# The order of VectorE's steps in a supertile of a two-layer graph network: weighting and part sums first, addition of finished sums behind them

## The chip, the cores and the metric

The kernel runs on one core of one Trainium2 chip. The metric is the device time of one execution in microseconds (us). The engines are TensorE (PE, its weight loads PEld), VectorE (DVE), ScalarE (ACT), GpSimd (POOL) and SyncE (SP). They run their own instruction queues and wait for each other by semaphores.

## The reference, cut to what matters

Two message-passing layers run over the same graph of 6250 nodes and 206250 edges, sorted by their destination `dst`. For each edge a row of its source node is taken, combined with four edge attributes (`sh`), scaled by a function of 16 edge scalars, and summed into the destination node:

```python
# layer 0, per edge
out_s = (einsum(xs[src] * es, W_ss) / sqrt(64) + einsum(xv[src], ev, W_vv) * ISQ3 / sqrt(32)) * ISQ2
out_v = (einsum(xs[src], ev, W_sv) * ISQ3 / sqrt(64) + einsum(xv[src], es, W_vs) * ISQ3 / sqrt(32)) * ISQ2
messages = concatenate([out_s, out_v]) * sigmoid(edge_scalars @ W_rad.T + b_rad)
agg = segment_sum(messages, dst)
# layer 1, per edge: h = silu(edge_scalars @ Wfc1), w = h @ Wfc2; e0, e1 = rows of the source
mid0 = w0 * e0 * sh0
mid1 = w3 * einsum(e1, sh1) / sqrt(3)
mid2 = w1 * e0 * sh1
mid3 = w2 * e1 * sh0
# segment means of them, then node products; each layer ends in a layer norm over 160 columns
```

All of it is float32.

## The kernel before, in words

The edges are cut into 404 supertiles of 512 (four tiles of 128, one edge to a partition). The weight products are made once for each node, ahead of the edges, in a table in DRAM: rows of 448 floats for layer 0, of 224 for layer 1. So an edge needs its source's row, weighted by its own attributes. The two edge layers are the same loop (`edge_layer`, L670 on VectorE, L929 on TensorE) with other bodies. A round is four supertiles; the loop runs over 101 rounds. What each engine does with supertile s:

- GpSimd (`gathers_of_round`, L370) gathers the rows: four indirect DMAs (L361), one for each tile, into one of four buffers (`rows0`, in the trace `arena`; `rows1`, in the trace `work`). It refills the buffer of supertile s with the rows of s + 4 when both ScalarE (`s_wtd`, L373) and VectorE (`s_wone`, L375) have weighted supertile s.
- ScalarE weights most of the row by the edge's attributes (L433, 12 instructions, `s_wtd`), when the messages of s - 2 are made (L441, L450), since they share a buffer; in layer 0 it then applies the sigmoid to TensorE's radial product (L459, `s_act`), in layer 1 the silu for s + 1 (L517). In layer 0 a part (`s_whead`) is done first, to which VectorE adds.
- TensorE waits for the messages of s (L947, L919), makes the radial product of s + 2 in layer 0 (L883, `s_lin`), and then sums the messages of s by destination (L907, `s_agg`): a matmul with a one-hot matrix of each tile over one window of 128 nodes, into one of two PSUM banks. In layer 1 the products for s + 1 and s + 2 (L900, L892) come ahead of the sums. Some supertiles have edges in further windows (about one in eight): `further` on both sides.
- VectorE turns the destinations into floats (L704), adds the sums that TensorE made of supertile s - 2 into `acc` (`add_sums`, L668; it waits for `s_agg`, L705), weights what ScalarE left (`weight_by_one`, L600: L609 in layer 0, L612 in layer 1, four instructions, `s_wone`), makes the one-hots (`select`, L657, L660, `s_oh`), and the messages (`messages0`, L616: two part sums at L625, then the product with the sigmoid's result at L632; `messages1`, L634: a part sum at L645, then L647, L648, L651, L652, L655). The last one signals `s_msg`.
- SyncE (`loads_behind`, L297) loads the small arrays: `escal` behind `s_lin`, `dst_sh` (destinations and attributes of two supertiles) behind the additions (L305), `srcs` once a round behind the gathers.

The order on each engine is written out by hand as the order of its queue; a wait holds up everything behind it on that engine. The sums of two supertiles have a bank each, the one-hots and the messages two buffers each, so a bank is added two supertiles behind its sums, ahead of the one-hots that reuse that buffer.

Of the kernel before, what the change touches and what calls it, by code (L numbers as in the profile page):

```python
# [6 lines left out]
MS, MV = 64, 32  # L7
# [33 lines left out]
DEEP0 = 2  # L41
# [6 lines left out]
def mk_gnn_resnorm_d2_gnn_r8_694f30_kernel(nc, a):  # L48
    f32, bf16, i32, i16 = mybir.dt.float32, mybir.dt.bfloat16, mybir.dt.int32, mybir.dt.int16
    ALU = mybir.AluOpType  # L50
# [3 lines left out]
    with ctx:  # L54
# [13 lines left out]
        msg0 = arena[:, at:at + 2 * TPS * MSG0].rearrange("p (s t c) -> p s t c", s=2, t=TPS)  # L68
# [6 lines left out]
        weighted1 = work[:, at1:at2].rearrange("p (s t c) -> p s t c", s=2, t=TPS)  # L75
        weighted0 = work[:, 0:DEEP0 * TPS * PARTS0].rearrange("p (s t c) -> p s t c", s=DEEP0, t=TPS)
# [37 lines left out]
        half = sb("half", [P, TPS, 2, MS])  # L114
# [29 lines left out]
        rad = [two_to_a_bank(2 * b, DIM) for b in range(2)]  # L144
# [37 lines left out]
        s_wtd = [sem(f"rows_weighted{l}") for l in range(2)]  # L182
# [373 lines left out]
        def _(dve):  # L556
# [43 lines left out]
            def weight_by_one(l, s, i, j):  # L600

                dve.wait_ge(s_rows[l][j], (i + 1) * 16 * TPS)
                if l == 0:
                    dve.wait_ge(s_whead, s + 1)
                for t in range(TPS):
                    scale = dst_sh[:, j, TPS + 4 * t + 2:TPS + 4 * t + 3]
                    if l == 0:
                        to = weighted0[:, j % DEEP0, t, 128:224]
                        last = nc.vector.scalar_tensor_tensor(to, rows0[:, j, t, 0:96], scale.bitcast(f32), to,  # L609
                                                              ALU.mult, ALU.add)  # L610
                    else:
                        last = nc.vector.tensor_scalar(weighted1[:, j % 2, t, 448:544], rows1[:, j, t, 128:224],  # L612
                                                       scale.bitcast(f32), None, ALU.mult)
                last.then_inc(s_wone[l], 1)

            def messages0(s, j):  # L616

                u, m, c = weighted0[:, j % DEEP0, :, :], msg0[:, j % 2, :, :], rad[j % 2]
                dve.wait_ge(s_wone[0], s + 1)
                dve.wait_ge(s_wtd[0], s + 1)  # L620

                def summed(to, at, k):

                    parts = u[:, :, at:at + k * P].rearrange("p t (k c) -> p t k c", k=k)
                    nc.vector.tensor_reduce(to, parts[:, :, :, 0:MS].rearrange("p t k c -> p t c k"),  # L625
                                            AX.X, ALU.add).then_inc(s_part[0], 1)

                summed(u[:, :, 0:MS], 160, 3)
                summed(u[:, :, MS:2 * MS], 224, 2)
                dve.wait_ge(s_part[0], s * 2 + 2)  # L630
                dve.wait_ge(s_act[0], s + 1)
                nc.vector.tensor_tensor(m[:, :, 0:DIM], u[:, :, 0:DIM], c, ALU.mult).then_inc(s_msg[0], 1)  # L632

            def messages1(s, j):  # L634


                u, m, w, h = weighted1[:, j % 2, :, :], msg1[:, j % 2, :, :], wps[j % 2], half

                def blocks(x, n):
                    return x.rearrange("p t (k c) -> p t k c", k=n)  # L640

                dve.wait_ge(s_wone[1], s + 1)
                dve.wait_ge(s_wtd[1], s + 1)

                nc.vector.tensor_tensor(h[:, :, 0, 0:MV], u[:, :, 224:256], u[:, :, 416:448], ALU.add).then_inc(s_part[1], 1)  # L645
                dve.wait_ge(s_w2, s + 1)
                nc.vector.tensor_tensor(m[:, :, 0:MS], u[:, :, 32:96], w[:, :, 0:64], ALU.mult)  # L647
                nc.vector.tensor_tensor(blocks(m[:, :, 96:192], 3), blocks(u[:, :, 0:288], 3)[:, :, :, 0:MV],  # L648
                                        bc(w[:, :, 128:160], 2, [P, TPS, 3, MV]), ALU.mult)
                dve.wait_ge(s_part[1], s * 2 + 1)  # L650
                nc.vector.tensor_tensor(h[:, :, 1, 0:MV], h[:, :, 0, 0:MV], u[:, :, 512:544], ALU.add).then_inc(s_part[1], 1)  # L651
                nc.vector.tensor_tensor(blocks(m[:, :, 192:384], 3), blocks(u[:, :, 256:544], 3)[:, :, :, 0:MS],  # L652
                                        bc(w[:, :, 64:128], 2, [P, TPS, 3, MS]), ALU.mult)
                dve.wait_ge(s_part[1], s * 2 + 2)
                nc.vector.tensor_tensor(m[:, :, 64:96], h[:, :, 1, 0:MV], w[:, :, 160:192], ALU.mult).then_inc(s_msg[1], 1)  # L655
# [14 lines left out]
            def edge_layer(l):  # L670
                LAST = NODE_TILES - 1
                waiting, newer = dve.alloc_register(f"window_to_add{l}"), dve.alloc_register(f"window_after{l}")
                waiting_more, visit = dve.alloc_register(f"more_to_add{l}"), dve.alloc_register(f"further_visit{l}")

                def held(register):
                    return dve.snap(register, min_val=0, max_val=LAST)  # L676

                dve.reg_mov(waiting, 0)  # L680
                dve.reg_mov(newer, 0)
                dve.reg_mov(waiting_more, 0)
                dve.reg_mov(visit, 1)
                dve.sem_inc(s_add[l], 1)
                dve.sem_inc(s_addx[l], 1)

                def next_visit():
                    return dve.snap(visit, min_val=1, max_val=SUPS * NODE_TILES)

                def further(s, j, window, k):  # L690
                    e = next_visit()
                    dve.wait_ge(s_aggx[l], e)
                    dve.wait_ge(s_addx[l], e)
                    dve.wait_ge(s_add[l], s + 2)
                    add_sums(l, MORE, held(waiting_more)).then_inc(s_addx[l], 1)
                    at = dve.snap(window + k + 1).with_bounds(min_val=1, max_val=LAST)
                    dve.reg_mov(visit, e + 1)
                    dve.wait_ge(s_addx[l], next_visit())
                    select(j, 2, at).then_inc(s_ohx[l], 1)
                    dve.reg_mov(waiting_more, at)  # L700

                def supertile(s, i, j, window, more):
                    dve.wait_ge(s_dsh[l][j // PAIR], (i + 1) * 16)
                    nc.vector.tensor_copy(dstf[:, j % 2, :], dst_sh[:, j, 0:TPS]).then_inc(s_dstf[l], 1)  # L704
                    dve.wait_ge(s_agg[l], s + 1)  # L705
                    dve.wait_ge(s_add[l], s + 1)
                    add_sums(l, FIRST + j % 2, held(waiting)).then_inc(s_add[l], 1)
                    weight_by_one(l, s, i, j)
                    dve.wait_ge(s_dstf[l], s + 1)
                    select(j, j % 2, window).then_inc(s_oh[l], 1)  # L710
                    (messages0, messages1)[l](s, j)
                    with dve.If(more > 0):
                        further(s, j, window, 0)
                        with dve.If(more > 1):
                            with dve.Fori(1, more) as k:
                                further(s, j, window, k)
                    dve.reg_mov(waiting, held(newer))
                    dve.reg_mov(newer, window)

                with dve.Fori(0, ROUNDS) as i:  # L720
                    _, values = nc.values_load_multi_w_load_instructions(  # L721
                        wtab[0:1, bass.ds(i, 1), 0:2, :], engines=[dve.engine], min_val=0, max_val=LAST,
                        skip_runtime_bounds_check_because="a dst is a node's number, so its window is one of the tiles")
                    for j in range(SLOTS):
                        supertile(i * SLOTS + j, i, j, values[j], values[SLOTS + j])

                for k, window in enumerate((waiting, newer)):
                    dve.wait_ge(s_agg[l], SUPS + k + 1)
                    dve.wait_ge(s_add[l], SUPS + k + 1)
                    add_sums(l, FIRST + k, held(window)).then_inc(s_add[l], 1)  # L730
                e = next_visit()
                dve.wait_ge(s_aggx[l], e)
                dve.wait_ge(s_addx[l], e)
                dve.wait_ge(s_add[l], SUPS + 3)
                add_sums(l, MORE, held(waiting_more)).then_inc(s_addx[l], 1)
                dve.reg_mov(visit, e + 1)
                dve.wait_ge(s_addx[l], next_visit())
                dve.sem_inc(s_done[l], 1)
# [426 lines left out]
```

## Time and profile before

| | |
|---|---|
| time, median of 3 runs | 5723.65 us (5711.29 to 5736.86) |
| the profiled execution's own time | 5735.73 us |
| its span, first to last instruction | 5733.9 us |
| mean granted TensorE clock | 0.699 of full speed |
| PE busy | 3993.3 us (70%) |
| DVE busy | 3889.5 us (68%) |
| ACT busy | 3382.4 us (59%) |
| POOL busy | 3141.9 us (55%) |

The span has a short opening, layer 0's edges up to about 2725 us, some 110 us of node work, layer 1's edges from about 2840 to 5650 us, and an end. The views below take 500 to 2600 us as a stretch of layer 0 and 3000 to 5500 us as a stretch of layer 1. Of a PE matmul the trace has the time at which it is taken up; its end is modelled. A row of a timeline gives the start, the time taken, engine and line, output and inputs, the count, and in brackets how long the engine was idle before it and who released it. "remote" is a release by an engine or a queue that the profile can't name.

### The profile page before, as it was taken

The numbers are of one execution on the slowest core, as the hardware profiler recorded it, in microseconds if no ns is written. First come the engines' busy times: TensorE is split into PE (matmuls) and PEld (weight loads), VectorE is DVE, ScalarE is ACT, GpSimd is POOL, SyncE is SP. The second block draws the span as 40 slices with busy tenths as digits, with TensorE's granted clock in tenths as the row PEclk, the third lists the DMA queues.
The fourth block names the chain that finished last, engine by engine and source line by source line (L and its number), as shares of the span: only waits on it lengthen the run. The fifth ranks groups of instructions, "written<-read, shape, count | busy, mean of one in ns | idle before, by whom it ended". The sixth has DMA issues, their size and how long they took to land.

```text
span 5733.9 us, 82997 instructions
## 1 busy us (share of the span) xinstructions
PE 3993.3 (70%) x16478; PEld 2635.1 (46%) x16479; DVE 3889.5 (68%) x12732; ACT 3382.4 (59%) x10841; POOL 3141.9 (55%) x3275
## 2 busy tenths in 40 slices
PE   5656565656566566666777777777777777777877
PEld 4445454545455455545544443444444344444435
DVE  4676777777777767777566666666666666666667
ACT  4666666666666666666555555555555555555555
POOL 4555555555555555555355555555555555555551
PEclk7555555555555555555888888888888888888888
DMA  7555555555555555555222222222222222222221
GB/s 239 150 147 154 148 152 148 152 148 154 146 150 152 148 151 148 151 149 133 79 76 76 75 74 74 73 75 74 75 73 74 76 76 78 75 74 76 77 76 51
DMA packets 325631, 641.98 MB, mean 112 GB/s; under 512 B 143598, under 2 KB 175131, under 8 KB 325499
## 3 DMA queue, kind: packets, MB, share of 16 engines
q0 software_dynamic: 181584, 557.89, 35.6%
q1 hardware_dynamic: 144016, 83.72, 5.6%
q8 instruction: 14, 0.23, 0.0%
q14 instruction: 17, 0.14, 0.0%
HBM read 620.47 MB, written 20.88 MB: 112 GB/s over the span
## 4 chain that ended last, share of the span: by engine, by line
PE 34%; DVE 28%; another core or an unknown queue 16%; issue 12%; ACT 6%; DVEq 3%; DMA 1%; ACTq 0%; POOL 0%; SPq 0%
PE ps L907 22%; DVE work L625 9%; DVE onehot L660 5%; ACT work L433 5%; DVE work L609 5%; PE ps L900 4%; PE ps L883 3%; PE ps L892 3%; DVE arena L632 1%; DVE work L612 1%; DVEq L676 1%; DVE work L648 1%; DVEq L721 1%; PE ps L870 1%
## 5 line engine op out<-in xcount | busy, mean ns | idle before, releaser
L361 POOL DMA_INDIRECT work<-table,srcs x1616 | 1559.9, 965 | 1237.8 <-issue 511.1
L361 POOL DMA_INDIRECT arena<-table,srcs x1616 | 1537.2, 951 | 1137.8 <-DVE work L609 619.3
L433 ACT ACTIVATE work<-arena,dst_sh 128x96 f32<-128x96 f32 (+1 forms) x4848 | 1415.7, 379 | 430.8 <-DVE arena L632 379.2
L907 PE MATMUL ps<-work,onehot 128*128 128x384 f32 x3616 | 1535.0, 578 | 180.6 <-DVE work L655 129.8
L433 ACT ACTIVATE work<-work,dst_sh 128x96 f32<-128x96 f32 (+1 forms) x4848 | 1499.6, 398 | 23.6 <-issue 10.8
L883 PE MATMUL ps<-wrad,escal 17*128 17x160 f32 x3232 | 561.2, 494 | 1033.9 <-DVE arena L632 857.5
L907 PEld LDWEIGHTS ps<-work,onehot 128*128 128x128 f32 x3616 | 771.3, 223 | 854.7 <-issue 524.7
L907 PE MATMUL ps<-arena,onehot 128*128 128x161 f32 x3616 | 1082.8, 479 | 12.3 <-issue 9.2
L907 PEld LDWEIGHTS ps<-arena,onehot 128*128 128x128 f32 x3616 | 925.0, 320 | 140.6 <-issue 131.2
L883 PEld LDWEIGHTS ps<-wrad,escal 17*128 17x128 f32 x3232 | 405.7, 309 | 1189.8 <-issue 840.6
L517 ACT ACTIVATE hid<-ps 128x256 f32<-128x256 f32 x404 | 152.0, 376 | 1180.6 <-remote 924.6
L660 DVE TENSOR_SCALAR onehot<-iota,dstf 128x128 f32 x3616 | 790.6, 287 | 16.4 <-issue 9.2
L900 PE MATMUL ps<-fc,hid 64*128 64x192 f32 x3232 | 422.9, 385 | 453.7 <-ACT hid L517 346.1
L668 DVE TENSOR_TENSOR arena<-arena,ps 128x384 f32 x455 | 251.1, 552 | 663.0 <-remote 320.2
L625 DVE TENSOR_REDUCE work<-work 128x256 f32<-128x768 f32 (+1 forms) x808 | 656.6, 854 | 0.0
L900 PEld LDWEIGHTS ps<-fc,hid 64*128 64x128 f32 x3232 | 290.4, 210 | 712.3 <-ACT hid L517 410.2
L459 ACT ACTIVATE ps<-ps 128x640 f32<-128x640 f32 x404 | 276.5, 684 | 563.0 <-remote 483.9
L668 DVE TENSOR_TENSOR acc<-acc,ps 128x161 f32 x455 | 145.7, 320 | 673.9 <-remote 340.0
L609 DVE SCALAR_TENSOR_TENSOR work<-arena,dst_sh,work 128x96 f32<-128x96 f32 x1616 | 406.3, 312 | 0.0
L652 DVE TENSOR_TENSOR work<-work,ps 128x768 f32<-128x768 f32 x404 | 382.2, 946 | 0.0
L612 DVE TENSOR_SCALAR work<-work,dst_sh 128x96 f32<-128x96 f32 x1616 | 337.4, 284 | 5.7 <-DMA work<-table,srcs 5.7
L632 DVE TENSOR_TENSOR arena<-work,ps 128x640 f32<-128x640 f32 x404 | 331.7, 821 | 14.0
(122 smaller groups left out, 2057.7 us busy)
## 6 DMA issues: line engine op xcount, KB each, us to landing
escal<-in_escal SPq DMA_DIRECT2D x404, 98.0 KB
arena<-table,srcs POOLq DMA_INDIRECT x1616
work<-table,srcs POOLq DMA_INDIRECT x1616
table<-work SPq DMA_DIRECT2D x49, 224.0 KB, 2.6
dst_sh<-in_dst_sh SPq DMA_DIRECT2D x404, 20.0 KB
table<-work SPq DMA_DIRECT2D x7, 784.0 KB, 4.0
acc<-in_xd SPq DMA_DIRECT2D x1, 3920.0 KB
arena<-in_xd SPq DMA_DIRECT2D x7, 560.0 KB, 4.1
```

Of the source, the lines that this page charges most:

```text
L361: pool.indirect_dma_start(out=rows[:, j, t, :], out_offset=None, in_=table, in_offset=bass.IndirectOffsetOnAxis(ap=srcs[:, b, j, t:t + 1], ...
L433: last = nc.scalar.activation(u[:, t, to:to + c1 - c0], r[:, t, c0:c1], ACT.Copy, scale=dst_sh[:, j, at:at + 1].bitcast(f32))
L609: last = nc.vector.scalar_tensor_tensor(to, rows0[:, j, t, 0:96], scale.bitcast(f32), to, ALU.mult, ALU.add)
L612: last = nc.vector.tensor_scalar(weighted1[:, j % 2, t, 448:544], rows1[:, j, t, 128:224], scale.bitcast(f32), None, ALU.mult)
L625: nc.vector.tensor_reduce(to, parts[:, :, :, 0:MS].rearrange("p t k c -> p t c k"), AX.X, ALU.add).then_inc(s_part[0], 1)
L632: nc.vector.tensor_tensor(m[:, :, 0:DIM], u[:, :, 0:DIM], c, ALU.mult).then_inc(s_msg[0], 1)
L652: nc.vector.tensor_tensor(blocks(m[:, :, 192:384], 3), blocks(u[:, :, 256:544], 3)[:, :, :, 0:MS], bc(w[:, :, 64:128], 2, [P, TPS, 3, MS]) ...
L660: last = nc.vector.tensor_scalar(onehot[:, b, t, :], iota[:, bass.ds(window * P, P)], dstf[:, j % 2, t:t + 1], None, ALU.is_equal)
L668: return nc.vector.tensor_tensor(to, to, bank(b)[:, 0:n], ALU.add)
L883: last = mm(rad[j % 2][:, t, :], escal[r, j, t % 2 * P:(t % 2 + 1) * P], wrad[r, :], start=True, stop=True)
L900: last = mm(wps[j % 2][:, t, :], hid[h, j % 2, t % 2 * P:(t % 2 + 1) * P], fc2[h, :], start=True, stop=True)
L907: last = mm(bank(to)[:, 0:(MSG0, MSG1)[l]], onehot[:, b, t, :], m[:, j % 2, t, :], start=t == 0, stop=t == TPS - 1)
```

## The change

Only VectorE's queue changes. `weight_by_one` and the first part of the messages, which is cut off as `parts0` (L618 to L629) and `parts1` (L642 to L645), go ahead of the wait for TensorE's sums. The new order in a supertile is: destinations as floats, weighting, part sums, addition of the sums of s - 2, one-hots, rest of the messages. The instructions, their operands, the semaphores and all other engines' queues are the same.

```diff
--- before.py
+++ after.py
@@ -613,9 +613,9 @@
                                                        scale.bitcast(f32), None, ALU.mult)
                 last.then_inc(s_wone[l], 1)
 
-            def messages0(s, j):
-
-                u, m, c = weighted0[:, j % DEEP0, :, :], msg0[:, j % 2, :, :], rad[j % 2]
+            def parts0(s, j):
+
+                u = weighted0[:, j % DEEP0, :, :]
                 dve.wait_ge(s_wone[0], s + 1)
                 dve.wait_ge(s_wtd[0], s + 1)
 
@@ -627,22 +627,28 @@
 
                 summed(u[:, :, 0:MS], 160, 3)
                 summed(u[:, :, MS:2 * MS], 224, 2)
+
+            def messages0(s, j):
+
+                u, m, c = weighted0[:, j % DEEP0, :, :], msg0[:, j % 2, :, :], rad[j % 2]
                 dve.wait_ge(s_part[0], s * 2 + 2)
                 dve.wait_ge(s_act[0], s + 1)
                 nc.vector.tensor_tensor(m[:, :, 0:DIM], u[:, :, 0:DIM], c, ALU.mult).then_inc(s_msg[0], 1)
 
+            def parts1(s, j):
+
+                u = weighted1[:, j % 2, :, :]
+                dve.wait_ge(s_wone[1], s + 1)
+                dve.wait_ge(s_wtd[1], s + 1)
+                nc.vector.tensor_tensor(half[:, :, 0, 0:MV], u[:, :, 224:256], u[:, :, 416:448], ALU.add).then_inc(s_part[1], 1)
+
             def messages1(s, j):
-
 
                 u, m, w, h = weighted1[:, j % 2, :, :], msg1[:, j % 2, :, :], wps[j % 2], half
 
                 def blocks(x, n):
                     return x.rearrange("p t (k c) -> p t k c", k=n)
 
-                dve.wait_ge(s_wone[1], s + 1)
-                dve.wait_ge(s_wtd[1], s + 1)
-
-                nc.vector.tensor_tensor(h[:, :, 0, 0:MV], u[:, :, 224:256], u[:, :, 416:448], ALU.add).then_inc(s_part[1], 1)
                 dve.wait_ge(s_w2, s + 1)
                 nc.vector.tensor_tensor(m[:, :, 0:MS], u[:, :, 32:96], w[:, :, 0:64], ALU.mult)
                 nc.vector.tensor_tensor(blocks(m[:, :, 96:192], 3), blocks(u[:, :, 0:288], 3)[:, :, :, 0:MV],
@@ -702,10 +708,11 @@
                 def supertile(s, i, j, window, more):
                     dve.wait_ge(s_dsh[l][j // PAIR], (i + 1) * 16)
                     nc.vector.tensor_copy(dstf[:, j % 2, :], dst_sh[:, j, 0:TPS]).then_inc(s_dstf[l], 1)
+                    weight_by_one(l, s, i, j)
+                    (parts0, parts1)[l](s, j)
                     dve.wait_ge(s_agg[l], s + 1)
                     dve.wait_ge(s_add[l], s + 1)
                     add_sums(l, FIRST + j % 2, held(waiting)).then_inc(s_add[l], 1)
-                    weight_by_one(l, s, i, j)
                     dve.wait_ge(s_dstf[l], s + 1)
                     select(j, j % 2, window).then_inc(s_oh[l], 1)
                     (messages0, messages1)[l](s, j)
```

## Rows read from the trace of the kernel before

**Rows 1.** Windows of both edge layers: us, busy us (instructions) of PE, PEld, DVE, ACT, POOL, clock, DMA.

```profile
500.00:2600.00 2100.00, 1286.30 (x5447) 1060.30 (x5447) 1486.20 (x4373) 1322.12 (x4181) 1220.94 (x1284) 0.53 0.55 150
3000.00:5500.00 2500.00, 1943.20 (x7528) 1019.77 (x7527) 1658.69 (x5967) 1430.40 (x4674) 1386.57 (x1436) 0.83 0.28 75
```

**Rows 2.** Waits of DVE, layer 0: waiter <- releaser: us in total, times, longest us.

```profile
DVE acc L668 <- remote: 272.7, 94, 7.7
DVE acc L668 <- PE ps L907: 244.1, 62, 5.5
```

**Rows 3.** Waits of DVE, layer 1.

```profile
DVE arena L668 <- remote: 283.6, 80, 7.7
DVE arena L668 <- PE ps L907: 240.9, 91, 5.1
...
DVE half L645 <- ACT work L433: 61.1, 44, 2.1
```

**Rows 4.** Timeline of layer 0, 1529 to 1543 us.

```profile
1529.40 1.44 PE L883 MATMUL ps<-wrad,escal 17*128 17x160 f32 x8 [1.63 <-DVE arena L632]
...
1530.76 2.52 PE L907 MATMUL ps<-arena,onehot 128*128 128x161 f32 x8
...
1535.85 0.95 POOL L361 DMA_INDIRECT arena<-table,srcs  x1 [0.30 <-issue]
1538.45 0.69 ACT L459 ACTIVATE ps<-ps 128x640 f32<-128x640 f32 x1 [5.64 <-remote]
1538.67 0.32 DVE L668 TENSOR_TENSOR acc<-acc,ps 128x161 f32 x1 [4.83 <-PE ps L907]
1538.91 1.00 DVE L609 SCALAR_TENSOR_TENSOR work<-arena,dst_sh,work 128x96 f32<-128x96 f32 x4
1539.05 3.49 ACT L433 ACTIVATE work<-arena,dst_sh 128x160 f32<-128x160 f32 x12
...
1539.82 0.87 DVE L660 TENSOR_SCALAR onehot<-iota,dstf 128x128 f32 x4
...
1540.61 1.63 DVE L625 TENSOR_REDUCE work<-work 128x256 f32<-128x768 f32 x2
1540.69 0.94 POOL L361 DMA_INDIRECT arena<-table,srcs  x1 [3.89 <-DVE work L609]
...
1542.27 0.82 DVE L632 TENSOR_TENSOR arena<-work,ps 128x640 f32<-128x640 f32 x1
```

**Rows 5.** Timeline of layer 0, 1614 to 1626 us.

```profile
1614.53 2.52 PE L907 MATMUL ps<-arena,onehot 128*128 128x161 f32 x8
...
1622.08 0.94 POOL L361 DMA_INDIRECT arena<-table,srcs  x1 [0.30 <-issue]
...
1625.15 0.32 DVE L668 TENSOR_TENSOR acc<-acc,ps 128x161 f32 x1 [7.56 <-remote]
```

**Rows 6.** Timeline of layer 1, 4215 to 4223 us.

```profile
4215.75 0.95 POOL L361 DMA_INDIRECT work<-table,srcs  x1 [0.30 <-issue]
...
4218.16 0.56 DVE L668 TENSOR_TENSOR arena<-arena,ps 128x384 f32 x1 [3.93 <-PE ps L907]
...
4220.23 1.02 POOL L361 DMA_INDIRECT work<-table,srcs  x1 [3.53 <-DVE work L612]
...
4222.20 0.28 DVE L655 TENSOR_TENSOR work<-half,ps 128x128 f32<-128x128 f32 x1
```

**Rows 7.** Waits of POOL, layer 0.

```profile
POOL arena L361 <- DVE work L609: 500.5, 217, 4.6
```

**Rows 8.** Waits of POOL, layer 1.

```profile
POOL work L361 <- DVE work L612: 341.0, 184, 4.3
POOL work L361 <- ACT work L433: 310.2, 99, 7.0
```

**Rows 9.** Waits of ACT, layer 0.

```profile
ACT ps L459 <- remote: 401.8, 102, 7.2
```

**Rows 10.** DMA issues of the page: count, KB each, us from issue to landing.

```profile
table<-work SPq DMA_DIRECT2D x49, 224.0 KB, 2.6
```

## The prediction, made before the change was run

> **What bounds the kernel now.** I read the view of windows first. Nothing is full in either edge layer: in layer 0 VectorE is busy 1486.2 of 2100 us and GpSimd's issuing 1220.9 us, in layer 1 TensorE 1943.2 of 2500 us [rows 1]. Four gathers go out for a supertile, so the issues count supertiles: 1284/4 = 321 in 2100 us (6.54 us each) and 1436/4 = 359 in 2500 us (6.96 us each). So a loop of waits bounds both layers.
>
> The waits of VectorE name its link. In layer 0 VectorE stands 272.7 + 244.1 = 516.8 us in 156 waits before L668, the addition of sums that TensorE made two supertiles before [rows 2]; in layer 1 it is 524.5 us in 171 waits, and the weighting by ScalarE makes it wait only 61.1 us at L645 [rows 3].
>
> The timeline says what kind of wait this is. The sums wanted at 1538.67 were in TensorE's queue at 1530.76 and by their record over at 1533.28, so the signal comes 5.4 us after the work. ScalarE's sigmoid wakes at 1538.45, for a product that began at 1529.40 and took 1.44. Two signals of different age arrive together. What comes before both is GpSimd's last gather issue at 1535.85: 2.8 us earlier [rows 4]. A second place: VectorE stands from 1617.59, GpSimd still has gathers to issue up to 1622.08, and the wait lasts 7.56 us, again until 3.1 us after the last issue, although the sums were over at 1617.05 [rows 5]. In layer 1 the last issue is at 4215.75 and the wait ends at 4218.16, 2.4 us later [rows 6]. I take it that TensorE's signals are **held back while a run of gathers goes on**, and come some 2.4 to 3.1 us after its last issue.
>
> GpSimd in turn stops because it has no permission: it wants the weighting of a supertile before it refills that buffer. It waits 500.5 us in 217 pauses on VectorE's L609 in layer 0 [rows 7]; in layer 1 it is 341.0 us in 184 pauses on L612 and 310.2 us in 99 on ScalarE [rows 8]. So the loop is: signal late, VectorE stands, no weighting, GpSimd stops, signal comes, VectorE weights, GpSimd goes on. The bookkeeping closes: 321 x 4 x 1.25 us (an issue of 0.95 and 0.30 between, [rows 4]) + 500.5 = 2106 of 2100 us, and 359 x 5.0 + 651.2 = 2446 of 2500 us.
>
> **The change, part by part.** No instruction is added or removed: 808 supertiles do the same work. Moved ahead of the wait on the sums are VectorE's weighting (1.00 us in layer 0, 0.80 in layer 1) and the part sums (L625, 1.63 us; L645, 0.28 us) with their waits on rows and on ScalarE.
>
> 1. Behind a late signal less is left. In layer 0 the addition starts at 1538.67 and the messages end at 1543.09: 4.42 us. Taken out: from 1538.91 to 1539.82 the weighting (0.91), from 1540.61 to 1542.27 the part sums (1.66). Left 1.85 us [rows 4]. In layer 1 it is 4.32 us (4218.16 to 4222.20 + 0.28) [rows 6], less 0.71 and 0.20, left 3.41. Upper bound of the gain: 2.57 and 0.91 us for each wait, 156 x 2.57 = 401 and 171 x 0.91 = 156 us in the two stretches. Lower bound: nothing, if the signal comes later by as much.
>
> 2. GpSimd's permission now comes before VectorE stands, so a run of gathers can be longer by one supertile (5.0 us), and by the reading above the signal is later by up to 5.0 us. The second place is the nearest row: with some 4.5 us of issues left the wait was 7.56 us instead of 4.83 or 3.93 [rows 4 to 6]. I take this in full.
>
> 3. The next permission comes later behind the signal. Now GpSimd resumes 1540.69 - 1538.67 = 2.0 us behind the addition [rows 4]. After: 1.85 us to the messages, 0.2 to the next supertile, 1.00 of weighting, 0.8 from its end to the issue (1539.91 to 1540.69): 3.85 us. Where ScalarE stood too, its sigmoid (0.69) and its 3.49 us of weights [rows 4] come first: about 4.4. ScalarE stands at the sigmoid in 102 of the waits [rows 9], so I take the mean, 4.1: a pause is 2.1 us longer. In layer 1: 3.41 + 0.2 + 0.80 + 0.8 = 5.2 instead of 2.1 (4218.16 to 4220.23), 3.1 us longer, but only at the 184 pauses that VectorE ends.
>
> 4. Fewer, longer pauses. Layer 0 has 321/217 = 1.48 supertiles to a pause of 500.5/217 = 2.31 us. One more for part 2, and 0.25 more because in a longer pause some sums get through that are held now (bounds: none, and every second one): 2.73. Then 321/2.73 = 118 pauses x 4.4 = 519 us against 500.5: +18, and for all 404 supertiles +23 us. Layer 1 has 359/283 = 1.27. Only the 184 of 283 pauses (0.65) get the further supertile: 1.27 + 0.65 + 0.25 = 2.17, 165 pauses x 4.31 us (0.65 x (341.0/184 + 3.1) + 0.35 x 310.2/99) = 711 against 651.2: +60, for 404 supertiles +68 us.
>
> 5. The rest lies beside other work. SyncE's loads of dst_sh wait for the addition, which now leaves 1.85 us instead of 4.4 to the messages that let ScalarE start on that buffer; the landing isn't shown, and the nearest row, 2.6 us for a store of 224 KB [rows 10], would cost ScalarE 0.8 us in every second supertile, hidden unless ScalarE is the last. Take 0; the upper end is 404 x 0.8 = 323 us, unlikely since ScalarE has over a third of its time idle [rows 1]. Its loads of escal and srcs behind it are rounds ahead. One-hots are later, but TensorE waits for the messages first and these still end the supertile. L645 now waits for ScalarE before the addition instead of behind it: 61.1 us of waiting [rows 3] lose their cover of 1.3 us each in 44 cases, 57 us at most, which I count in rival C. All GpSimd and VectorE durations are taken as they are.
>
> Sum: 23 + 68 = +91 us on the profiled execution's 5735.73 us: 5827. That execution is 12 us above the median of the runs, 5723.65, so against the median 5815; I say **5815 us**.
>
> The Trainium skill ("SBUF — State Buffer", section Who interferes with whom) speaks against part 2: it says that a DMA never contends with a compute engine and that only VectorE and GpSimd share a port. By that rule gathers can't delay TensorE's signals and rival A is the outcome. Rows 4 to 6 show signals that come together and behind the last issue, which that rule doesn't explain.
>
> **Rivals.** A, the plain gain: the signals are late by themselves and GpSimd's issues have no part in it. Then the whole of part 1 comes off: 401 x 404/321 = 505 us and 156 x 404/359 = 176 us, at most 681; the shortest waits are shorter than 2.57 us, so about 600: 5125 us. For it: the wait in rows 4 is longer than the work moved. Against it: the wait of 7.56 us, and three waits that end so alike behind GpSimd's last issue.
>
> B, faster through fewer pauses. Same mechanism, but in the longer pause after a signal (GpSimd starts 3.85 to 5.2 us behind it) the next sums get through nearly always: the messages are there at 1.85 us, product and sums take 1.44 + 2.52 us [rows 4], so 5.8 us in layer 0. It decides for this when more than about one in two gets through. With each one: layer 0 1.48 + 2 = 3.48, 92 pauses x 4.4 = 405, -95 us, for the layer -120; layer 1 1.27 + 0.65 + 1 = 2.92, 123 x 4.31 = 530, -121, for the layer -136. 5724 - 256 = 5470 us. Against it: GpSimd has begun again before 5.8 us.
>
> C, slower by more: none gets through (2.48 and 1.92 supertiles to a pause). 129 x 4.4 = 568, +67, +85 for the layer; 187 x 4.31 = 806, +155, +174 for the layer. With 57 us for L645: 5724 + 85 + 174 + 57 = 6040 us.
>
> **Chances.** Own forecast 0.45 (range 5690 to 5930), A 0.13, B 0.22, C 0.20. Faster or slower means beyond 0.5%, or 29 us, which is about what a measurement of this kernel can tell. Faster: A, B and a hair of the own range (0.02): 0.37. Same: 0.11, all of it in the own range. Slower: 0.32 of the own, and C: 0.52. The range leaves out A and a few of C's worst: 5400 to 6030 us.
>
> **What the profile after would show.** Part 1: from the addition to the messages' end 1.85 us in layer 0 and 3.4 in layer 1. Part 2: VectorE's waits before L668 still end 2.4 to 3.1 us behind GpSimd's last issue, and in layer 0 are as long as now or longer, but fewer. Parts 3 and 4: GpSimd's pauses number some 120 instead of 217 in 2100 us and last over 4 us. Wrong if the waits before L668 shrink to under half with GpSimd's runs grown together (A), or if the pauses are fewer than 100 (B). Waiting at L645 or L609 on ScalarE of over 150 us would speak for C.

## The result, and the profile after

The changed kernel takes **5915.8 us** (median of 4 runs, 5898.4 to 5952.0), beside 5717.5 us for the kernel before (5707.6 to 5736.9): ratio 1.034 [1.032, 1.037], +198 us. The direction is as forecast and the time lies in the range of 5400 to 6030 us, but the forecast +91 us are less than half of the +198 measured. The profiled executions differ by less: 5898.35 - 5735.73 = +162.6 us, as that of after is the lowest of its runs (17 us under their median) and that of before 18 us above its own.

Where the time went, from the start of the first messages to the end of the last in each layer (worked out from the two traces; in layer 1 up to the last messages' first product, L647 before and L653 after): layer 0 2628.5 us before and 2721.0 after, **+93**; layer 1 2799.7 and 2871.0, **+71**. The sum, +164, is the whole difference of the profiled executions. Forecast were +23 and +68.

The windows of both layers, as in [rows 1]:

```profile
500.00:2600.00 2100.00, 1228.04 (x5282) 1011.90 (x5284) 1428.69 (x4240) 1267.02 (x4044) 1190.62 (x1244) 0.54 0.53 145
3000.00:5500.00 2500.00, 1914.16 (x7364) 1004.48 (x7364) 1654.82 (x5840) 1392.09 (x4569) 1348.59 (x1406) 0.83 0.28 73
```

1244 issues are 311 supertiles (6.75 us each, 6.54 before), 1406 are 351.5 (7.11 us, 6.96 before). Every engine is less busy: more waiting, not more work. The granted clock is what it was. VectorE's waits in layer 0 answer to [rows 2], to which a third group of the kernel before belongs: waits for which the profile shows no releaser ("issue"). It comes first here:

```profile
DVE acc L668 <- issue: 21.8, 9, 3.1
```

```profile
DVE acc L674 <- remote: 478.8, 82, 10.6
DVE acc L674 <- issue: 72.8, 18, 7.4
DVE work L625 <- remote: 36.9, 18, 4.7
DVE acc L674 <- PE ps L914: 28.4, 13, 2.8
```

The waits before the addition (now L674) are fewer and longer: 580.0 us in 113 instead of 516.8 + 21.8 = 538.6 in 165, up to 10.6 us instead of 7.7. GpSimd's waits in layer 0, to be held against [rows 7]:

```profile
POOL arena L361 <- issue: 506.3, 1082, 7.9
POOL arena L361 <- DVE work L609: 345.2, 104, 9.1
POOL arena L361 <- ACT work L433: 35.1, 43, 8.0
```

Part of the pauses is now in the first group (its longest is 7.9 us, though the common gap is 0.30). Counted in the trace from 500 to 2700 us as the time above the usual 1.25 us from issue to issue, where it is over 0.35 us, 220 pauses of 2.31 us became **130 of 4.25 us** (124 to 140 with a limit of 0.5 or 0.3 us; before the limit makes no difference). ScalarE, against [rows 9]:

```profile
ACT ps L459 <- remote: 673.7, 90, 14.2
```

One place in the timeline of layer 0 shows the new order at work, with a signal on time and one held:

```profile
1519.31 0.32 DVE L674 TENSOR_TENSOR acc<-acc,ps 128x161 f32 x1
1519.54 0.88 DVE L666 TENSOR_SCALAR onehot<-iota,dstf 128x128 f32 x4
...
1520.32 0.82 DVE L636 TENSOR_TENSOR arena<-work,ps 128x640 f32<-128x640 f32 x1
...
1528.27 0.94 POOL L361 DMA_INDIRECT arena<-table,srcs  x1 [0.30 <-issue]
1528.38 0.32 DVE L674 TENSOR_TENSOR acc<-acc,ps 128x161 f32 x1 [4.57 <-remote]
...
1531.29 0.69 ACT L459 ACTIVATE ps<-ps 128x640 f32<-128x640 f32 x1 [4.81 <-remote]
1531.51 1.00 DVE L609 SCALAR_TENSOR_TENSOR work<-arena,dst_sh,work 128x96 f32<-128x96 f32 x4
...
1533.30 0.95 POOL L361 DMA_INDIRECT arena<-table,srcs  x1 [4.09 <-DVE work L609]
```

From the addition to the messages' end are 1520.32 + 0.82 - 1519.31 = 1.83 us, 4.42 before. The sigmoid at 1531.29 comes 3.0 us behind the last issue, as in [rows 4 to 6]; the addition at 1528.38 got its signal sooner, within 0.1 us of that issue. So the hold isn't strict: some signals slip through. GpSimd stands 4.09 us until it is given the weighting of 1531.51.

The end of a matmul is modelled, so these rows alone can't tell a late signal from late work. ScalarE's end is measured, and its signal is held too. Here its weighting is over at 1503.92 + 3.49 = 1507.41, and VectorE, which waits for it before the part sums, starts at 1513.33, together with ScalarE's sigmoid and 3.0 us behind the last gather issue:

```profile
1503.92 3.49 ACT L433 ACTIVATE work<-arena,dst_sh 128x160 f32<-128x160 f32 x12
...
1510.32 0.95 POOL L361 DMA_INDIRECT arena<-table,srcs  x1 [0.30 <-issue]
...
1513.33 1.03 DVE L625 TENSOR_REDUCE work<-work 128x256 f32<-128x768 f32 x1 [4.70 <-remote]
1513.42 0.69 ACT L459 ACTIVATE ps<-ps 128x640 f32<-128x640 f32 x1 [6.01 <-remote]
```

The update of ScalarE's semaphore is recorded 0.09 us before VectorE starts, 5.8 us behind the end of the work. So what is late is the signal, and not TensorE's alone. From 500 to 2600 us, 61 recorded updates of this semaphore are over 0.3 us late, 22 in the kernel before.

VectorE's and GpSimd's waits in layer 1, against [rows 3] (again with the third group of before, which comes first) and [rows 8]:

```profile
DVE arena L668 <- issue: 59.9, 36, 5.1
```

```profile
DVE arena L674 <- remote: 254.7, 54, 8.0
DVE half L643 <- ACT work L433: 224.5, 109, 6.8
DVE work L653 <- remote: 178.5, 49, 7.5
...
DVE half L643 <- issue: 43.8, 28, 4.4
DVE arena L674 <- PE ps L914: 28.5, 18, 3.1
DVE arena L674 <- issue: 18.2, 10, 4.7
```

```profile
POOL work L361 <- ACT work L433: 419.4, 93, 7.2
POOL work L361 <- DVE work L612: 156.9, 77, 8.6
```

Here the wait moved. Before the addition it fell from 524.5 + 59.9 = 584.4 to 254.7 + 28.5 + 18.2 = 301.4 us, but L643 (L645 before) now waits 224.5 us for ScalarE instead of 61.1. ScalarE waits for another product of TensorE's, held in the same way. In the timeline the last issue is at 4212.72, and ScalarE (L517) and VectorE's L653 wake together 2.8 to 2.9 us behind it:

```profile
4212.72 0.96 POOL L361 DMA_INDIRECT work<-table,srcs  x1 [0.30 <-issue]
...
4215.56 0.42 DVE L653 TENSOR_TENSOR work<-work,ps 128x256 f32<-128x256 f32 x1 [1.40 <-remote]
4215.62 0.38 ACT L517 ACTIVATE hid<-ps 128x256 f32<-128x256 f32 x1 [7.57 <-remote]
...
4220.49 0.95 POOL L361 DMA_INDIRECT work<-table,srcs  x1 [6.82 <-ACT work L433]
```

### The profile page after: what moved, and what is told of

The parts are those of the page before. It is cut to its first block, busy times and chain, and to the rows that moved or that the text cites. A ratio compares the mean times of both kernels' runs of the same rounds, so it can differ in the third digit from the quotient of the medians.

```text
span 5896.5 us, 82593 instructions
## 1 busy us (share of the span) xinstructions
PE 3989.1 (68%) x16478; PEld 2623.5 (44%) x16479; DVE 3909.9 (66%) x12732; ACT 3360.6 (57%) x10841; POOL 3142.8 (53%) x3275
## 4 chain that ended last, share of the span: by engine, by line
another core or an unknown queue 32%; ACT 29%; DVE 13%; issue 12%; PE 11%; DVEq 1%; DMA 1%; ACTq 0%; POOL 0%; SPq 0%; POOLq 0%
ACT work L433 27%; PE ps L914 5%; DVE onehot L666 3%; DVE work L609 3%; DVE work L625 2%; PE ps L907 2%; PE ps L899 2%; DVE arena L636 1%; ACT ps L459 1%; ACT hid L517 1%; PE ps L877 1%; DVE acc L674 1%; DMA dst_sh<-in_dst_sh 0%; PE ps L1090 0%
## 5 line engine op out<-in xcount | busy, mean ns | idle before, releaser
L914 PE MATMUL ps<-arena,onehot 128*128 128x161 f32 x3616 | 1069.7, 475 | 14.7 <-issue 11.9
L517 ACT ACTIVATE hid<-ps 128x256 f32<-128x256 f32 x404 | 152.1, 376 | 1264.0 <-remote 1099.7
L666 DVE TENSOR_SCALAR onehot<-iota,dstf 128x128 f32 x3616 | 826.5, 301 | 16.5 <-issue 6.1
L907 PE MATMUL ps<-fc,hid 64*128 64x192 f32 x3232 | 438.3, 397 | 564.4 <-ACT hid L517 538.1
L674 DVE TENSOR_TENSOR acc<-acc,ps 128x161 f32 x455 | 143.7, 316 | 756.1 <-remote 637.1
L674 DVE TENSOR_TENSOR arena<-arena,ps 128x384 f32 x455 | 250.5, 551 | 340.5 <-remote 276.4
L643 DVE TENSOR_TENSOR half<-work 128x128 f32<-128x128 f32 x404 | 121.1, 300 | 352.3 <-ACT work L433 260.3
```

The lines of the kernel that those rows point to most:

```text
L666: last = nc.vector.tensor_scalar(onehot[:, b, t, :], iota[:, bass.ds(window * P, P)], dstf[:, j % 2, t:t + 1], None, ALU.is_equal)
L674: return nc.vector.tensor_tensor(to, to, bank(b)[:, 0:n], ALU.add)
L907: last = mm(wps[j % 2][:, t, :], hid[h, j % 2, t % 2 * P:(t % 2 + 1) * P], fc2[h, :], start=True, stop=True)
L914: last = mm(bank(to)[:, 0:(MSG0, MSG1)[l]], onehot[:, b, t, :], m[:, j % 2, t, :], start=t == 0, stop=t == TPS - 1)
```

## The experiments

The theory: while GpSimd issues gathers, the engines' semaphore signals are held, TensorE's above all; the new order gives GpSimd its permission before VectorE stands, which makes the runs of gathers longer. Ratios are to the kernel before, run beside it on the same chip, with 95% intervals. "Loops" are the two times from first to last messages, 2628.5 and 2799.7 us before. Where no interval stands, the number is a single run.

**1. One layer at a time.** The new order in layer 0 alone (e1_layer0), then in layer 1 alone (e2_layer1, with `l == 1`):

```diff
+                    if l == 0:
+                        weight_by_one(l, s, i, j)
+                        (parts0, parts1)[l](s, j)
                     dve.wait_ge(s_agg[l], s + 1)
                     dve.wait_ge(s_add[l], s + 1)
                     add_sums(l, FIRST + j % 2, held(waiting)).then_inc(s_add[l], 1)
-                    weight_by_one(l, s, i, j)
+                    if l != 0:
+                        weight_by_one(l, s, i, j)
```

> The new order in layer 0 only; layer 1 as before. Theory H (TensorE's signals are held back while GpSimd issues gathers, and VectorE's early weighting lets GpSimd issue on): the traces of before and after put layer 0's edges at 2628 and 2721 us, so +93 us, some 5810 us, with the waits before the addition ending 2.4 to 3.5 us behind a last gather issue. Rival (the new order costs through SyncE's late loads of dst_sh, 88 us of ScalarE's waiting in the stretch of layer 0): the same time, but the wait on dst_sh carries it.

> The new order in layer 1 only. The traces put layer 1's edges at 2800 and 2871 us, so +71 us, some 5790 us. If the two layers didn't add up, something outside the loops would be at work. Theory H: GpSimd's pauses on VectorE fall from 184 to some 80 in 2500 us. Rival: L643, the part sum ahead of the addition, now waits on ScalarE (224.5 us against 61.1) and carries the loss.

Measured: e1_layer0 5819.6 us, 1.015 [1.011, 1.018], loops 2712.5 and 2782.0; e2_layer1 5816.3 us, 1.014 [1.011, 1.017], loops 2630.7 and 2870.7. Each layer pays, in its own loop: +84 and +71. The two together are 1.028, a little less than 1.034; the rest stays open. The rival of the second, that the wait for ScalarE ahead of the addition (L643) carries the loss, falls with experiments 2 and 3.

**2. The weighting ahead, the part sums not** (e3_weights_ahead). GpSimd's permission is as early as in the changed kernel, but more is left behind the signal:

```diff
+                    weight_by_one(l, s, i, j)
                     dve.wait_ge(s_agg[l], s + 1)
...
-                    weight_by_one(l, s, i, j)
                     dve.wait_ge(s_dstf[l], s + 1)
                     select(j, j % 2, window).then_inc(s_oh[l], 1)
+                    (parts0, parts1)[l](s, j)
                     (messages0, messages1)[l](s, j)
```

> Only the weighting goes ahead of the wait on the sums; the part sums stay behind the one-hots. GpSimd's permission is as early as in the changed kernel, the wait on ScalarE is not. Theory H: still slower than before in both layers, as the permission is what harms: 5800 to 5950 us. Rival (the part sums' wait on ScalarE ahead of the addition harms): at or below 5720 us.

Measured: 6012.8 us, 1.047 [1.042, 1.052], loops 2778.1 (+150) and 2922.1 (+122). Its waits of VectorE in layer 0:

```profile
DVE acc L674 <- remote: 482.1, 89, 12.1
DVE acc L674 <- PE ps L914: 96.2, 23, 7.8
```

The early weighting is what harms, and the part sums ahead are the good half of the change: 6012.8 - 5915.8 = 97 us across two measurements, or 1.2% of the time by the ratios. The loss is above the expected 5800 to 5950 us. In layer 1 it is +122 us although no part sum stands ahead of the addition, so the wait for ScalarE there isn't what costs.

**3. The new order without the early permission** (e4_permission). GpSimd also waits for the addition before it refills a buffer:

```diff
                         pool.wait_ge(s_wtd[l], s + 1)
+                        pool.wait_ge(s_add[l], s + 2)
+                        pool.sem_inc(s_pool, 1)
```

> The changed kernel, with one more wait on GpSimd: it refills a buffer only when VectorE's addition of that supertile is done too (value s + 2 of the additions' semaphore), so that the permission comes behind TensorE's signal again, as before the change, and still 0.2 us after the addition instead of 2.0. Theory H: the signal is released one supertile earlier, VectorE has 1.85 us instead of 4.4 left behind it, GpSimd goes on sooner: faster than before, 5150 to 5500 us. Rival A (GpSimd's issues have no part in the delay): a wait more can only cost, 5900 us or above.

Measured: 5615.5 us, **0.978** [0.976, 0.981]; loops 2500.1 (-128) and 2808.8 (+9). With one wait *more* the same order is faster than either kernel, by 118 us. The gain is short of the expected 5150 to 5500 us, since layer 1 gives none. But layer 1 loses none either, though VectorE waits 284.4 us for ScalarE at the part sum there (L645 of this run; 224.5 us at L643 of the changed kernel, which lost 71 us): again it isn't that wait which costs, but the early permission. Waits of VectorE and of GpSimd in layer 0:

```profile
DVE acc L676 <- remote: 426.9, 101, 6.5
...
DVE acc L676 <- PE ps L916: 20.6, 9, 3.0
```

```profile
POOL arena L361 <- DVE acc L676: 384.4, 128, 5.4
```

The longest wait is 6.5 us again instead of 10.6, and a pause is 384.4/128 = 3.0 us. In its timeline ScalarE and VectorE wake 3.3 us behind the last issue, and GpSimd goes on 1.1 us behind the addition, 2.0 before [rows 4]:

```profile
1501.79 0.95 POOL L361 DMA_INDIRECT arena<-table,srcs  x1 [0.30 <-issue]
...
1505.10 0.69 ACT L461 ACTIVATE ps<-ps 128x640 f32<-128x640 f32 x1 [2.47 <-remote]
1505.13 0.32 DVE L676 TENSOR_TENSOR acc<-acc,ps 128x161 f32 x1 [5.29 <-remote]
...
1506.24 0.94 POOL L361 DMA_INDIRECT arena<-table,srcs  x1 [3.51 <-DVE acc L676]
```

**4. That in layer 0 alone, layer 1 as before** (e9_layer0_permission): both edits under `if l == 0`.

> The new order and GpSimd's permission behind the addition in layer 0 only; layer 1 entirely as before. The run with the permission in both layers had layer 0's edges at 2500 us and layer 1's at 2809, against 2628 and 2800 before: so 5710 - 128 = some 5590 us, the best so far. If the layers influenced each other (clock), it would miss by over 0.5%.

Measured: **5590.0 us**, 0.975 [0.973, 0.978], loops 2489.9 (-139) and 2797.0 (-3). The best version where signals are held.

**5. Is it the gathers at all?** No gathers after the first round (e5_no_gathers):

```diff
-                        gather(l, j, b)
```

(and every wait on s_rows is for the first 16 * TPS). It weights the same rows again and again; the two runs behind it and the plain loads of experiment 6 read other rows or fewer columns than the reference. They serve for timing alone. Then the two queues exchanged (e6_rows_by_sp): SyncE loads each buffer in plain blocks of 128 rows, as many bytes as the gathers, and GpSimd issues SyncE's small loads.

```diff
+                    for t in range(TPS):
+                        sp.dma_start(rows[:, j, t, :], table[(j * TPS + t) * P:(j * TPS + t + 1) * P, :]).then_inc(s_rows[l][j], 16)
```

Then gathers of 160 floats instead of 448 in layer 0 (e7_small_rows), from xd instead of the table:

```diff
+                        out=rows0[:, j, t, 0:DIM], out_offset=None, in_=a["xd"],
```

> The kernel before, in its old order, with GpSimd's gathers left out after the first round (the same rows are weighted again and again; GpSimd keeps its waits). Theory H: without gathers TensorE's signals come with the end of its work; VectorE's waits before L668 nearly vanish in layer 0 (under 60 us in 2100 us of the loop instead of 517), a supertile takes 4.5 to 5.0 us, layer 0's edges some 1950 us. Rival A (the signals are late by themselves): the waits before L668 stay at over 1 us a supertile.

> The kernel before, in its old order, with the queues exchanged: SyncE loads the same number of rows into the same buffers at the same permission (plain loads of 128 consecutive rows of the table instead of gathers by index), and GpSimd issues the small loads that were SyncE's. It tells GpSimd's issuing apart from the bytes. Theory H1 (GpSimd's issuing of gathers holds the signals): TensorE's signals are on time, the waits before L668 fall under 100 us a stretch. Theory H2 (the traffic of the rows holds them, whoever issues it): the waits stay where they are, some 500 us in 2100 us.

> The kernel before, in its old order; in layer 0 the gathers after the first round take 160 floats a row, from x, instead of 448 from the table (the rest of the row keeps older values). As many issues, 0.36 of the bytes. H1: layer 0 takes as long as before, 2628 us. H2: the waits before L668 shrink with the bytes; layer 0 falls well below 2628 us, to 2100 to 2400 us. Layer 1, left alone, is the control.

Measured, beside 5731 us for the kernel before: e5_no_gathers 4245.0, e6_rows_by_sp 4230.8, e7_small_rows 5725.9 us, with layer 0's loop at 1952, 1955 and 2617 us. The window of 500 to 2000 us and VectorE's wait before the addition, first for e6_rows_by_sp:

```profile
500.00:2000.00 1500.00, 1207.35 (x5246) 996.55 (x5248) 1411.07 (x4214) 1267.14 (x4025) 213.92 (x388) 0.55 0.66 203
```

```profile
DVE acc L678 <- PE ps L917: 4.9, 11, 0.6
```

and for e7_small_rows:

```profile
500.00:2000.00 1500.00, 920.50 (x3901) 759.86 (x3902) 1064.21 (x3132) 946.57 (x2995) 877.18 (x921) 0.54 0.23 60
```

```profile
DVE acc L677 <- PE ps L916: 205.4, 51, 5.6
DVE acc L677 <- remote: 161.5, 43, 7.6
```

(The kernel before has 164.0 and 207.4 us there.)

Without the indexed gathers VectorE is busy 1411 of 1500 us and hardly waits, though *more* bytes move (203 GB/s, 150 in [rows 1]). With them, and 60 GB/s, it waits as ever. It isn't the number of bytes.

**6. The queue or the indices?** GpSimd issues plain loads of 128 rows in place of the gathers (e13_plain_by_pool, e15_plain_by_pool_again, e18_plain_by_pool_third, one kernel on three chips); and the exchanged queues in the new order (e10_sp_new_order).

```diff
-                    pool.indirect_dma_start(
...
+                    pool.dma_start(rows[:, j, t, :], table[(j * TPS + t) * P:(j * TPS + t + 1) * P, :]).then_inc(s_rows[l][j], 16)
```

> The kernel before, in its old order, with GpSimd issuing plain loads of 128 consecutive rows in place of the gathers by index, as many and as large. Theory H1a (any DMA issued by GpSimd in a row holds TensorE's signals): VectorE's waits before L668 stay at over 300 us in 2100 us of layer 0. H1b (only the indexed gathers do, whose descriptors take the 0.95 us): the waits vanish and the time is near 4230 us.

> The run with the rows loaded by SyncE (4231 us, waits before L668 of 4.9 us in 1500 us of layer 0) in the new order. It shows what the move is worth where TensorE's signals are on time. Theory H: there is no wait left that the moved work could fill, so 4200 to 4260 us; a gain over 1% would mean that the plain gain exists and is only eaten by the hold, a loss over 1% that the order harms by itself.

Measured: 4225.5 and 4262.0 us. But on that chip (chip 3) the kernel *before* itself took **4398.1 us** (21 runs, 4390.5 to 4402.4), and no signal of TensorE's was late in the traces taken there, with gathers (e11_dst_sh_early, e8_dst_sh_best) or without. So neither number tells anything about the hold. The second is 0.7% above the 4230.8 us of the old order on chip 4 and 2 us above the expected 4200 to 4260: no gain, and no loss over 1%. Chip 10 is like chip 3 (4390.6 us for the kernel before, 24 runs); on chip 11 it takes 5724.0 us.

> GpSimd issues plain loads of 128 rows in place of the indexed gathers, old order. On a chip with late signals: H1a (any row of DMA issues by GpSimd holds TensorE's signals) keeps the waits before L668, over 300 us in 2100 us of layer 0; H1b (only the indexed gathers do) gives some 4225 us, as on the chip with signals on time.

> GpSimd issues plain loads of 128 rows in place of the indexed gathers, old order. If the kernel before takes some 5725 us beside it: H1a (any DMA issued by GpSimd holds the signals) keeps the waits before L668, over 300 us in 2100 us of layer 0; H1b (only the indexed gathers do) gives some 4225 us.

Measured: 4231.6 us on chip 10 and **4230.8 us on chip 11**, where the kernel before takes 5724.0. Window and wait of the latter:

```profile
500.00:2000.00 1500.00, 1205.64 (x5253) 995.07 (x5251) 1411.83 (x4220) 1268.95 (x4030) 659.35 (x1240) 0.55 0.66 203
```

```profile
DVE acc L666 <- PE ps L905: 4.1, 9, 0.6
```

The same engine issues as many loads of as many bytes to the same buffers, and nothing is held. The runs of issues are shorter (four take 2.1 us instead of 5.0), but that doesn't explain it: in the trace of before, of the TensorE updates whose matmul ended in the first 2.1 us of a run of gathers, 50 of 137 came late; here none of 93 did (500 to 2000 us, sums and radial products). So it is the gathers, and not GpSimd's issuing of DMA as such, that hold the signals. The edit changes three things at once, though: the loads have no index, their rows are consecutive, and an issue is shorter. Which of them counts isn't shown.

**7. The changed kernel where signals are on time** (e14_changed_again, chip 10):

> The changed kernel itself, beside the kernel before on the same chip. On a chip where the kernel before takes some 5725 us (signals late): ratio 1.03 again. On one where it takes some 4400 us (signals on time): Theory H says that nothing is left to fill or to hold, ratio 0.995 to 1.005; the rival (the order costs by itself, through ScalarE's weights or dst_sh) says over 1.01 there too.

Measured: 4395.5 us against 4390.6, 1.001 [1.000, 1.002]. Window and waits from 500 to 2000 us:

```profile
500.00:2000.00 1500.00, 1154.15 (x5036) 952.48 (x5034) 1348.45 (x4037) 1214.90 (x3861) 1138.38 (x1188) 0.55 0.70 194
```

```profile
DVE work L625 <- ACT work L433: 124.4, 145, 1.2
```

No wait stands before L674. GpSimd sets the pace with 1188/4 = 297 supertiles of 5.05 us, that is 4 x 1.25 us of issuing. The order in itself is neutral here, where GpSimd's issues leave nothing to gain; it costs only where signals are held.

**8. The load of dst_sh.** Part 5 took it as nothing. SyncE waits for the weighting instead of the addition, in the changed kernel (e11_dst_sh_early on chip 3, e16_dst_sh_again on chip 10, e19_dst_sh_third on chip 11) and in the version of e9_layer0_permission (e8_dst_sh_best on chip 3, e17_best_again on chip 10):

```diff
-                        sp.wait_ge(s_add[l], s + PAIR + 2)
+                        sp.wait_ge(s_wone[l], s + PAIR)
```

> The changed kernel with one wait replaced: SyncE loads dst_sh of the next round's pair when VectorE has weighted the pair's last supertile, no longer when a later addition is done. In the changed kernel ScalarE waits 88 us in 59 waits on that load in 2100 us of layer 0. If that wait is on the loop's path, some 100 us come back: 5815 us. Theory H (the loop is GpSimd's permission and TensorE's held signals; ScalarE's short waits on dst_sh lie beside it): at most 40 us, 5880 us or above.

> The best version so far (new order and permission behind the addition in layer 0, layer 1 as before; ratio 0.975) with the same early load of dst_sh, where ScalarE waits 70 us in 44 waits on it in 1500 us of layer 0. Theory H: here the loop is tighter and ScalarE's weights end the supertile more often: 10 to 80 us faster, 5510 to 5580 us. If nothing, ScalarE isn't on the path here either.

> The changed kernel with SyncE's load of dst_sh released by VectorE's weighting. On a chip with late signals: at most 40 us better than the changed kernel beside it by Theory H; some 100 us if ScalarE's wait of 88 us in 2100 us of layer 0 is on the path. On a chip with signals on time: the same as the changed kernel.

> New order and permission behind the addition in layer 0, layer 1 as before, with the early dst_sh. On a chip with late signals: 5510 to 5590 us, ratio 0.963 to 0.977 (0.975 without the early dst_sh). On a chip with signals on time: 1.002.

> The changed kernel with SyncE's load of dst_sh released by VectorE's weighting. If the kernel before takes some 5725 us beside it: Theory H says 5880 us or above (ratio over 1.027), the rival (ScalarE's wait for dst_sh is on the path) 5815 us or below (ratio under 1.016). If it takes some 4395 us: ratio 1.000.

Measured: e11_dst_sh_early 4399.6 us, 1.000 [0.999, 1.001]; e16_dst_sh_again 4392.8, 1.000 [0.999, 1.001]; e8_dst_sh_best 4405.9, 1.002 [1.001, 1.003]; e17_best_again 4400.8, 1.002 [1.001, 1.003]. Where signals are held, e19_dst_sh_third took 5936.8 us, 1.036 [1.034, 1.039], no better than the changed kernel's 1.034, although ScalarE's wait for the load (88.2 us in 2100 us of layer 0 of the changed kernel) is gone from the trace. The load isn't on the path. The other four runs can't tell this, since nothing is held on chips 3 and 10. With the early load the version of e9_layer0_permission was not run on a chip that holds signals; where they are on time it costs 0.2%, which includes its extra wait.

## Why the mechanism was right and the size wrong

**The step that failed is part 4 of the prediction, for layer 0:** the 0.25 supertiles more to a pause, "because in a longer pause some sums get through". The runs show about none: 2.5 supertiles to a pause instead of 2.73, and +93 us instead of +23. The rest of this section takes the steps in turn.

**The reading of the bound held.** Experiments 3, 5 and 6 show it: without gathers the waits before the addition are gone. Of the sums' semaphore, the trace of before has 217 updates from 500 to 2000 us (some are missing, 230 sums ended); 46 of them, 21%, came within 0.3 us of their matmul's modelled end. In e14_changed_again, e6_rows_by_sp and e18_plain_by_pool_third all did (297, 309 and 310). Where the late ones come: from 500 to 2600 us of before, sums and radial products have 426 updates over 0.3 us late. 371 of them fell behind the last issue of a run of gathers, 329 of these 2.0 to 3.6 us behind it. After, it is 335, 292 of them behind a last issue, mostly 2.4 to 4.0 us. And in both traces all matmuls of five TensorE semaphores that ended over 3.2 us behind any gather issue were signalled on time (227 before, 273 after). The Trainium skill ("SBUF — State Buffer", section Who interferes with whom) has it that a DMA doesn't contend with a compute engine. For bytes the runs agree: 203 GB/s of plain loads held nothing. For the gathers on chips 6, 4 and 11 they don't, and there the measurement decides. That section is on the ports of SBUF; whether the hold has to do with a port, no run here shows.

**Part 1** held to the hundredth: from a late addition to the messages' end the median is 1.84 us in layer 0 (1.85 forecast) and 3.5 in layer 1, most often 3.40 (3.41). **Part 2** held: GpSimd's runs of gathers in layer 0 were mostly 4 (96) and 8 (94), and are mostly 12 (56), 4 (23 to 27, by the limit of a pause) and 16 (19 to 21). Experiments 2 and 3 show that this is the harm. **Part 3** held: behind a wait of over 1 us GpSimd resumes at a median of some 4.15 us instead of 2.03, and a pause is 4.25 us long (4.4 forecast).

**Part 4 failed for layer 0.** The 0.25 was nothing: 326 supertiles by 130 pauses are 2.5, which is the prediction's own lower bound of 2.48. By that bound the layer's cost was +85 us, and +93 was measured; the "+23" came of 0.25 supertiles per pause alone. Of the 93, the pauses make (552/326 - 508/337) x 404, some 75 us; the rest lies in slightly longer steps within the runs. With +85 in place of +23 the sum would have been 153 against the 163 of the profiled executions.

**Layer 1's +68 was right by luck, by two errors.** The forecast had 283 pauses become 165 in 2500 us. Counted in the traces, as above with a limit of 0.4 us, they were 213 of 3.36 us in 390 supertiles (2900 to 5600 us) and became 198 of 3.92 us in 379 (2960 to 5660 us), where 4.31 was forecast. The waits of [rows 8] included 130 of under 0.4 us, about the plain gap between issues, which are no pauses. So the pauses hardly became fewer, and were lengthened by less than forecast. They still account for all of the +71: 198 x 3.92/379 = 2.05 us a supertile instead of 213 x 3.36/390 = 1.84. The 224.5 us at L643 are past the 150 us that were named as a sign for rival C, but experiments 2 and 3 show that this wait isn't the cost. Nor was C's price right for this layer, +174 and 57 us. So layer 0 went as C, layer 1 by its size as the forecast, not by its steps. And the range ended at 6030 us, below the 6040 that C itself gave.

**Rival A** fell where signals are held; on chips 3 and 10, with nothing to gain, the order is neutral. **Rival B** (sums get through in the longer pause) fell with the 0.25. In experiment 3, with the permission behind the addition, a pause on it comes only every 1338/4/128 = 2.6 supertiles and is 3.0 us long; that this is what B meant isn't shown.

Between 163 and 198 us lies the spread of the runs, as said above. Open: why the two layers alone make 1.028 and together 1.034, why layer 1 gains nothing from experiment 3, what in a gather holds the signals, and why on some chips alone.

## What to carry to other kernels

When unrelated engines wake at one moment, look for what ended just before on an engine that neither waits for. Work taken from behind a late signal is only a gain if it doesn't also give another engine leave to run ahead: move the work, and keep the permission where it was. Count pauses as gaps above the usual gap, not as rows of waits.

## What the runs showed of the hardware

- Runs of GpSimd's indexed gathers held signals of TensorE's, up to 13 us behind the modelled end of the matmul (13.34 at most in the trace of before, in layer 1), and fewer of ScalarE's (5.8 us in the rows above, behind a measured end). Plain loads by GpSimd or SyncE, of the same bytes, held none. Gathers of 160 floats held as those of 448 (longest wait 7.6 and 7.7 us).
- The hold was there on some chips. Chips 4, 6 and 11 ran the kernel before in 5724 to 5734 us (medians of 7 runs each), chips 3 and 10 in 4398 and 4391 (of 21 and 24), and no run on a chip was of the other kind. The chip of the main measurement isn't on record; by its 5717.5 us it is of the first kind. Each chip was measured once, so whether it is the chip or a state it was in isn't shown. Where there is no hold, the gathers still cost 4398 - 4226 = 172 us (chip 3), most likely since their issues set the pace: 0.95 us and 0.30 between, where a plain load took 659.35/1240 = 0.53 us of GpSimd.
- So a change that costs 3.4% where signals are held costs 0.1% where they aren't, and the best version of the one (0.975) is no gain on the other (1.002 with the early load of dst_sh; without it, it wasn't run there).
